# Graph layers on one core: edge weights moved into one-hot matrices, one PSUM bank for each tile of nodes, and GpSimd copying its own row indices

## What is computed

```python
# layer 0: graph attention over the edges, batch norm, residual, layer norm  -> x1
# layer 1: two graph convolutions
h   = segment_sum(dinv[src] * w * dinv[dst] * (x1 @ W1)[src], dst)      # 256 wide, loop g1
h2  = segment_sum(dinv[src] * w * dinv[dst] * (h)[src], dst) @ W2       # 256 wide, loop g2
# layer 2: mean of the neighbours
a   = segment_sum(w * x2[src], dst) / deg                               # 512 wide, loop g3
# layer 3: sums in the other direction
out = segment_sum(w * support[dst], src)                                # 512 wide, loop g4
```

## Time and profile before

| | |
|---|---|
| Median of 3 timed runs | 4099.45 us (4093.15 to 4100.37) |
| Span of the profiled execution | 4580.2 us |
| PE busy | 3028.5 us, 66% |
| POOL busy | 2891.1 us, 63%, 3191 instructions |
| DVE busy | 2534.5 us, 55% |
| ACT busy | 1784.3 us, 39% |
| Moved by DMA | 520.84 MB, mean 114 GB/s |

### The profile page before, as it was taken

One profiled execution on the slowest core, in us unless ns is written; L12 is line 12 of the kernel. 1 busy time (PEld: TensorE's weight loads), 2 busy tenths in 40 slices (PEclk: granted clock), 3 DMA queues, 4 the chain that ended last, 5 costly groups with the idle time before them and its releaser, 6 DMA issues. The chain is left out here.

```text
span 4580.2 us, 63826 instructions
## 1 busy us (share of the span) xinstructions
PE 3028.5 (66%) x11605; PEld 1656.8 (36%) x11606; DVE 2534.5 (55%) x4864; ACT 1784.3 (39%) x3995; POOL 2891.1 (63%) x3191
## 2 busy tenths in 40 slices
PE   7566665377677665655545556686777799577773
PEld 6344443244444243333323333342222244222221
DVE  8455554666666663434433444574555654565656
ACT  3111111366666563333323333334444433344444
POOL 5666666666666666666666666676666667566662
PEclk8777776688999886667656666798999999899997
DMA  3211111355555153323243332335666611566653
GB/s 101 74 45 63 48 60 39 116 168 163 162 162 162 47 154 88 87 87 89 86 137 87 88 88 86 72 72 171 175 172 174 173 50 42 143 173 176 174 170 124
DMA packets 207412, 520.84 MB, mean 114 GB/s; under 512 B 63334, under 2 KB 70638, under 8 KB 206892
## 3 DMA queue, kind: packets, MB, share of 16 engines
q0 software_dynamic: 157600, 413.73, 31.9%
q1 hardware_dynamic: 49714, 105.90, 7.5%
HBM read 475.94 MB, written 43.49 MB: 113 GB/s over the span
## 5 line engine op out<-in xcount | busy, mean ns | idle before, releaser
L1639 PE MATMUL g_part<-g_rows,g_hot 128*128 x3328 | 1549.2, 614 | 864.7 <-ACT g_rows L1560 499.7
L1615 DVE TENSOR_TENSOR k_acc<-k_acc,g_part 128x256 f32 (+1 forms) x1664 | 920.5, 553 | 1073.0 <-PE g_part L1639 350.2
L1639 PEld LDWEIGHTS g_part<-g_rows,g_hot 128*128 128x128 f32 x3328 | 749.4, 243 | 1664.4 <-issue 1596.2
L1560 ACT ACTIVATE g_rows<-g_rows,k_rec 128x256 f32<-128x256 f32 (+1 forms) x1176 | 663.8, 577 | 1096.6 <-PE g_part L1639 255.0
L1223 POOL DMA_INDIRECT at_rows<-h_table,at_index x392 | 390.9, 997 | 249.7 <-ACTq L1249 132.5
L1285 PE MATMUL at_part<-at_rows,at_hot 128*128 x832 | 401.0, 567 | 187.8 <-DVE at_hot_first L1299 68.9
L1580 POOL DMA_INDIRECT g_rows<-support,g_index x392 | 379.3, 968 | 220.6 <-issue 120.7
L1580 POOL DMA_INDIRECT g_rows<-x_scaled_w,g_index x392 | 383.3, 978 | 212.3 <-issue 121.8
L1580 POOL DMA_INDIRECT g_rows<-hidden_scaled,g_index x392 | 380.7, 971 | 214.6 <-issue 139.6
L1580 POOL DMA_INDIRECT g_rows<-x,g_index x392 | 380.3, 970 | 210.3 <-issue 112.9
L673 POOL DMA_INDIRECT edges_by_dst<-fr_records,f_dst_slots x392 | 384.1, 980 | 167.6 <-issue 166.8
(11 more groups left out here) (409 smaller groups left out, 3705.1 us busy)
## 6 DMA issues: line engine op xcount, KB each, us to landing
f_rows<-low_rows SPq DMA_DIRECT2D x28, 896.0 KB
x<-n_out SPq DMA_DIRECT2D x50, 256.0 KB
f_x_in<-in_x SPq DMA_DIRECT2D x25, 256.0 KB
h_table<-f_h SPq DMA_DIRECT2D x25, 256.0 KB
gat_h_all<-h_table SPq DMA_DIRECT2D x5, 1280.0 KB
n_x<-in_x SPq DMA_DIRECT2D x25, 256.0 KB
n_x<-x SPq DMA_DIRECT2D x25, 256.0 KB
support<-k_acc SPq DMA_DIRECT2D x25, 256.0 KB
```

What stands on the lines that cost most here:

```text
L1560: act.activation(rows[:, n, :], rows[:, n, :], ACT.Copy, scale=col(rec[:, :, R_W], g * BT + (h * BT + n))).then_inc(weighed, 1)
L1615: dve.tensor_tensor(here, here, part[u % RING][:, 0:width].unsqueeze(1), ALU.add).then_inc(added, 1)
L1639: pe.matmul(part[u % RING][:, 0:width], hot[:, u % (2 * HOTS), :], rows[:, bass.ds(place[n], 1), :].rearrange("p o f -> p (o f)"), start=T ...
```

## The change

- **Weights.** The one-hot matrix holds the edge's weight instead of 1: VectorE makes it for one pair at a time with one instruction of two operations (compare, multiply), 16 matrices ahead (8 in g4). ScalarE no longer touches the rows. For this the weight of an edge must stand in the pair's column, so `attention_weights` and `Records` spread `R_W` by a product with `sel`, as they do for `R_LOCAL`.
- **PSUM.** Node tile t has bank t % 4. TensorE clears the four banks with a product of zeros, ScalarE writes the first value into a bank (what `acc` holds, or zeros where `keep=False`, in g3 and g4), all pairs of the node tile add to it, and ScalarE copies it to `acc` when the node tile's last pair is summed (`T_ENDS`, 25 new numbers in the tables) and opens the bank for node tile t + 4. VectorE's additions are gone, and both clearings of `acc`.
- **Row indices.** GpSimd copies eight indices itself at the start of each half of eight edge tiles, and waits for its own copy.
- **Handing on.** SyncE takes over the waits on landed rows and summed pairs. It increments `arrived` for TensorE and `freed` for GpSimd.

The core of the diff:

```diff
-def aggregate(nc, k, name, rec, pairs, table, width, acc, fetch=(), source=None):
-    RING, HOTS, HALVES = 8, 4, EC // BT
+def aggregate(nc, k, name, rec, pairs, table, width, acc, fetch=(), source=None, keep=True):
+    RING, HALVES = 16 if source is None else 8, EC // BT
...
             @block.sync
+                held = [sp.alloc_register(f"{s.name}_done{n}") for n in range(BT)]
+                sp.sem_inc(freed, BT - LAG)
+                def half(g, h):
+                    done = at_least_one(sp, held, registers(nc, mybir.EngineType.SP, pairs, T_DONE, g * BT + h * BT, 1,
+                                                            TILES + 2 * BT))
+                    for n in range(BT):
+                        sp.wait_ge(gathered[n], g * 16 + (h + 1) * 16)
+                        sp.sem_inc(arrived, 1)
+                        sp.wait_ge(summed, done[n])
+                        sp.sem_inc(freed, 1)
...
+            @block.gpsimd
+                def half(g, h):
+                    pool.tensor_copy(index[:, h, :], col(other, g * BT + h * BT, BT)).then_inc(indexed, 1)
+                    pool.wait_ge(indexed, g + (h + 1))
+                    for n in range(BT):
+                        pool.wait_ge(freed, g * BT + (h * BT + n + 1))
+                        pool.sem_inc(granted, 1)
+                        pool.indirect_dma_start(rows[:, n, :], None, table, ...)
...
             @block.scalar
-                        act.activation(rows[:, n, :], rows[:, n, :], ACT.Copy, scale=...).then_inc(weighed, 1)
+                def open_bank(t):
+                    here = part[:, t % BANKS, 0:width]
+                    begin = act.copy(here, acc[:, t, 0:width]) if keep else act.activation(here, zero, ACT.Copy, scale=0.0)
+                    begin.then_inc(opened if t else opened_first, 1)
+                for t in range(NT):
+                    act.wait_ge(summed, ends[n])
+                    act.copy(acc[:, t, 0:width], part[:, t % BANKS, 0:width]).then_inc(evicted, 1)
+                    if t + BANKS < NT:
+                        act.wait_ge(evicted, t + 1)
+                        open_bank(t + BANKS)
...
             @block.vector
+                def mark(j, n):
+                    dve.tensor_scalar(hot[:, n, :], k.columns[:, 0:P], col(rec[:, :, R_LOCAL], j), col(rec[:, :, R_W], j),
+                                      ALU.is_equal, ALU.mult).then_inc(hot_ready, 1)
...
             @block.tensor
+                for b in range(BANKS):
+                    last = pe.matmul(part[:, b, :], k.ones[0:1, :], blank[:, :], start=True, stop=True, ...)
...
+                        tile = node_tiles(nc, mybir.EngineType.PE, pairs, at)
+                            pe.wait_ge(opened, turn[n])
-                            pe.matmul(part[u % RING][:, 0:width], hot[:, u % (2 * HOTS), :],
-                                      rows[:, bass.ds(place[n], 1), :], start=True, stop=True).then_inc(summed, 1)
+                            pe.matmul(part[:, bass.ds(tile[n] % BANKS, 1), 0:width], hot[:, u % RING, :],
+                                      rows[:, bass.ds(place[n], 1), :], start=False, stop=True, ...).then_inc(summed, 1)
...
# gcn_output, prepare: the clearing of acc goes
-            return act.activation(acc[:, bass.ds(t, 1), 0:F], k.ones[:, 0:1]..., ACT.Copy, scale=0.0)
```

More of the change, by code:

```diff
@@ L63 @@
 ATT = 2 * HEADS + 1
+BANKS, T_ENDS = 4, TILES_PAD
 SC_EACH = 4
@@ L907, in sums @@
             last.then_inc(self.summed, 1)
+        ends = self.banks[2][0:1, EC:EC + NT]
+        pe.matmul(ends, self.w.pair[:, 0, self.here], self.k.ident[0:NT, 0:NT], start=True, stop=False, skip_group_check=True)
+        pe.matmul(ends, self.k.ones[0:1, 0:1], self.k.columns[0:1, 2 * BT:2 * BT + 1].broadcast_to([1, NT]),
+                  start=False, stop=True, skip_group_check=True).then_inc(self.summed, 1)
     def needs(self, dve):
@@ L1500, in known @@
         dve.wait_ge(self.copied, 1)
[L1503 to L1509 removed]
+def aggregate(nc, k, name, rec, pairs, table, width, acc, fetch=(), source=None, keep=True):
+    RING, HALVES = 16 if source is None else 8, EC // BT
     with Scope(nc, name) as s:
         rows = s.sb("rows", [P, BT, width])
+        hot = s.sb("hot", [P, RING, P])
+        blank = s.sb("blank", [1, F])
         index = s.sb("index", [P, 2, BT], I32)
[L1513 to L1514 removed]
+        part = s.ctx.enter_context(nc.psum_tensor(f"{name}_part", [P, BANKS, F], FP))
         gathered = [s.sem(f"gathered{n}") for n in range(BT)]
[L1516 to L1521, removed]
+        arrived, freed = s.sem("arrived"), s.sem("freed")
+        hot_ready, summed = s.sem("hot_ready"), s.sem("summed")
+        blank_made, blanked, opened_first, opened, evicted = (
+            s.sem(n) for n in ("blank_made", "blanked", "opened_first", "opened", "evicted"))
+        fetched = s.sem("fetched")
+        records = None
+        if source is not None:
+            banks = [s.ps(f"pt{i}", [P, F]) for i in range(4)]
+            records = Records(k, s, source, rec, pairs, banks, rows[0:ROWS_T, BT - LAG:BT, 0:TILES])
         other = rec[:, :, R_ROW].bitcast(I32)
[L1523 removed]
+        indexed, granted = s.sem("indexed"), s.sem("granted")
         def halves(eng, half):
@@ L1618, in _ @@
+                for n in range(RING):
+                    mark(n, n)
+                with dve.Fori(1, TILES // RING) as i:
+                    for n in range(RING):
+                        if n % 4 == 0:
+                            dve.wait_ge(summed, i * RING + (2 * BT + n - RING + 4))
+                        mark(i * RING + n, n)
             @block.tensor
@@ L1621, in _ @@
                     records.turn(pe)
+                pe.wait_ge(blank_made, 1)
+                for b in range(BANKS):
+                    last = pe.matmul(part[:, b, :], k.ones[0:1, :], blank[:, :], start=True, stop=True, skip_group_check=True)
+                last.then_inc(blanked, 1)
+                pe.wait_ge(opened_first, 1)
+                pe.wait_ge(opened, BANKS - 1)
                 pe.sem_inc(summed, 2 * BT)
-                pe.sem_inc(added, RING)
                 held = [pe.alloc_register(f"{s.name}_need{n}") for n in range(BT // 2)]
+                turn = [pe.alloc_register(f"{s.name}_turn{n}") for n in range(BT)]
                 with pe.Fori(0, TILES // BT // 2) as i:
```

139 lines of the change are left out of this document (58 added, 81 removed).

## The result

The changed kernel takes 4235.54 us (median of 4 runs, 4232.89 to 4240.10), the kernel before 4099.57 us beside it (4093.15 to 4100.37): a ratio of 1.0335, with a 95% interval of 1.0320 to 1.0349, so 136 us slower. The forecast was 4242 us. All medians and ratios here are those of fast runs: one execution of 6526 us of the kernel with GpSimd's copies alone and one of 8409 us of the kernel that copies ahead, both slow, are left out.

A forecast was written before the change was run, and what follows sets the result against it. The prediction took GpSimd's queue of gathers, 1.25 us apart, to bound the timed loops; its terms, +147 - 4 + 4 - 5 + 1 + 0 = +143 us on 4099.45, gave 4242 us, range 4060 to 4350 us.

The forecast's parts named there:

- The premise on the silences: Gather loops: stretches where several engines fall silent, 465.8 us of GpSimd's waits, belong to the recording, mostly absent when timed.
- first step: Timed gather loops are GpSimd's 392 steps of 1.25 us; wrong if its 333 us of `freed` waits and the time shrink.
- Part 1: Row indices: 196 copies moved onto GpSimd's queue cost 0.75 us each, +147 us (+135 to +161).
- Part 2: Handing on by SyncE: 0 us in the loops, -1 us at each loop's end, -4 us.
- Part 3: Loop starts: opening the banks puts TensorE's first pair 9 us in, covered by eight gathers; +4 us (0 to +12).
- Part 4: Clearings of `acc` dropped: -5 us (0 to -11) in g4, nothing gained in `gcn_output`.
- Part 6: VectorE beside gathers: -34 us without old matrices, +31 to +78 from scalar operations; taken as 0 (-34 to +50).
- The handing on was real: Rival: `freed` waits exist in timed runs and SyncE removes them in part; 4018 us at three quarters; chance 0.17.
- The copy is nearly free: Rival: GpSimd's sequencer goes on while each copy runs, 0.20 us each; 4134 us; chance 0.10.
- TensorE the bound: Rival: TensorE sets the pace in g3 and g4 at 1.45 us a tile, +86 us, 4328 us; chance 0.08.
- No difference: Rival: GpSimd's step has slack in timed runs that the profile hides; time within 0.2%; chance 0.04.
- VectorE locks GpSimd out: Rival: scalar operations between SBUF tensors hold up gathers for their whole 0.28 us, +331 us, about 4540 us; chance 0.05.

The follow-up runs named there:

- the loop with only gathers: Loop g2 of the kernel after with VectorE copying the row indices, GpSimd only the first four halves; 4085.94 us, ratio 0.9968 to the kernel before.
- the second profile of after: The kernel after, unchanged, run once more beside the kernel before: 4230.88 us against 4097.44, ratio 1.0327.

## Why the prediction was right, and where it was not

**The premise on the silences** was right in that they are absent from the timed runs it added to, and unfounded in its cause. On two of three chips every execution is as long as the profiled one (4595 and 4503 us), and on the third the profiled ones are as short as the others. The match of 465.8 us of waits with the 480.8 us that the profiled execution had over the timed runs says that the two are the same time, not what makes it. The prediction read that no engine's work explains the silences, from three engines that resume together (all three with "issue" named, not two of them); all three wait, directly or through `freed`, for TensorE's increments. In the silence that it shows, the waits of ScalarE and of VectorE end in the same moment, at 2520.92, and of the two VectorE waits for no landing. The profile of before has the loop lengths of the chip of 4595 us, and its times are those of the chip of 4097 us; that it came from such a chip is argued, not shown. By the prediction's own sign its first step is wrong: the long waits for `freed` are gone from the profile after. In the two profiles of after only four to eight gaps a loop, besides those behind copies, are over 0.5 us. The step that was built on it, GpSimd's 1.25 us as the pace of the timed loop, holds: 392 x 1.254 = 492 us, and the loop with only gathers takes 497.

**Part 1**, the term that carries the sum, was +147 us; the copies alone measured +149.1 us. 0.79 us each lies inside the 0.69 to 0.82 us read from the node steps. The prediction left open whether the copy or its wait costs; the copy issued ahead shows the wait.

**Part 2**: no gain from SyncE in the loops, as far as the kernel in which SyncE alone was changed shows it, on a chip with silences. The start was mis-sized. The prediction saw that SyncE issues its eight loads first in g2 and charged nothing for it. The increment of `freed` stands behind them, and the first gather waits 6.98 us for it in the second profile of after:

```profile
2102.45 2.87 SPq L1554 DMA_DIRECT2D wc_b<-in_b  x1
2106.23 0.99 POOL L1582 DMA_INDIRECT g_rows<-hidden_scaled,g_index  x1 [6.98 <-SPq L1556]
```

From the last gather of g1 to the first of g2 are 35.6 us, against 29.7 in the kernel with GpSimd's copies alone: +5.8 us.

**Part 3** gave +4 us on the reason that eight gathers, 10 us, cover the opening. That reason failed twice. Only four are out, as `freed` begins at 4: the fifth gather stood 3.14, 2.43, 4.46 and 9.41 us in the four loops of the second profile of after, 19.4 us against 6.8 with the copies alone. And eight would not cover it but in g2: TensorE's first pair comes 10.7, 7.3, 12.0 and 16.9 us after the first gather, and with the increment moved ahead the ninth gather stands instead. The first eleven gaps of the loops cost 11.4 us more than with the copies alone, near the end of the range of 0 to 12. All gaps over 0.5 us inside halves come to 39.5 us less the ordinary 0.30, against 22.8 us with the copies alone: +17 us.

**Part 4**: from the last gather of g2 to the first of g3 198.0 us, against 197.6: nothing gained in `gcn_output`, as forecast. From g3 to g4 230.9 against 231.6. For the clearing in g4 -5 us were forecast; in the kernel with the copies alone the first eleven gaps of g4 cost 4.1 us more than those of g1, so there was no more than that to gain, and the opening of the banks took it.

**Part 6** took 0 from -34 to +50 us. The gathers went from a mean of 0.969 us (copies alone) to 0.952, 1568 x 0.0168 = -26 us: the old matrices' cost is gone and the new ones add little, though one takes 0.361 us and not the estimated 0.28. The old matrices' 22 ns a gather were read rightly: in the kernel before with scalar operations in their place, the only change, the mean fell from 0.970 to 0.947 us. Gaps behind copies are also shorter by 8 us in all. So -26 - 8 + 17 + 6 = -11 us, and the two profiled spans differ by 4228.9 - 4239.7 = -10.8 us (the medians by -16). Two errors, a start that costs more and a neighbour that costs less, nearly cancelled. That the sum came within 7 us of the time is luck to this extent.

**The rivals.** *The handing on was real*: not on the chip of 4097 us, where those waits do not exist, and not by SyncE where they do. *The copy is nearly free*: true of a copy, not of one whose result is awaited. *TensorE the bound*: no; g3 runs in 505 us without copies. *No difference*: this is close to what the copies alone did on the chip of 4595 us, +0.4%, by another mechanism than the one given. *VectorE locks GpSimd out*: no. 1664 scalar operations of 0.36 us ran beside gathers whose mean is 0.954 us, 0.005 above the median of 0.949. In the second profile of after the 632 gathers with such an operation beside them have a mean of 0.957 us and the others 0.949; the longest takes 1.06 us. Of the operations that begin during a gather a few are held, up to 0.58 us against the usual 0.34. The scatter of 5.88 us, which the prediction read as a sign of the lock, is none: the last scatter before g2 takes 5.88 or 5.89 us in all 14 profiles, beside operations of 0.34 and 0.47 us. The Trainium skill, page "SBUF — State Buffer", section "Who interferes with whom", says that `tensor_scalar` can take the shared port pair when its operands allow it, and that whoever comes second is then fully blocked. No run shows whether these operations took it; a block for their whole length is not to be seen here.

## What to carry to other kernels

An instruction on the engine that sets the pace costs its wait, not its busy time: a 0.20 us copy whose result is awaited at once cost 0.79 us, issued six gathers ahead 0.07 us, and on an engine with time to spare nothing. When a profiled span and the timed runs differ by 12%, they may come from different chips: profile again and compare spans before a difference is given to the recording. When an engine waits for two things at once, the name that the profile gives is a guess: look for another engine that waits for only one of them, as VectorE does here. Count how much work can be out before the first hand-over (four gathers by the semaphore, eight by the buffers) against the whole start of a loop, since raising the first number alone only moved the wait to the second.

## What the runs showed of the hardware

- The same kernel took 4097, 4503 and 4595 us on three chips, each steady within 0.5%. The difference is in TensorE's increments that come late, several at once. Whether it belongs to the chip or to its condition at that hour is open. So is the part of the recording: the nine profiles with silences hold 26,000 to 27,400 updates of semaphores, the five without them 64,800 to 65,200, and every execution has at least its span and clock noted.
- On a chip with silences the changes hardly count, or in the other direction: +0.4% for copies that cost 3.6% elsewhere, and +0.5% for the kernel that gains 0.3% elsewhere.
- GpSimd pauses 0.9 to 2.5 us before the 114th, 220th and 326th gather of each loop, 106 apart, in the five profiles without silences. The waits name "issue" or the increment of `freed` there. Its cause is open.
